# A gated recurrence on one Trainium2 core: level-0 fill ahead of the output step, output matrices in two buffers, output product in bank A

## What is computed

```python
def step(carry, inp):
    S, R = carry
    q_t, k_t, v_t, a_t, aR_t, b_t, g_t = inp
    kn = k_t / jnp.maximum(jnp.linalg.norm(k_t, axis=-1, keepdims=True), 1e-12)
    pred = jnp.einsum('bhji,bhj->bhi', S, kn)
    r = jnp.clip(v_t - pred, -CLIP, CLIP)
    S = a_t[..., None] * S
    kp = jnp.einsum('bhd,bhde->bhe', kn, S)
    S = S + b_t[..., None, None] * kn[..., None] * (v_t - kp)[..., None, :]
    o = jnp.einsum('bhji,bhj->bhi', S, q_t)
    R = aR_t[..., None] * R
    kpR = jnp.einsum('bhd,bhde->bhe', kn, R)
    R = R + g_t[..., None, None] * kn[..., None] * (r - kpR)[..., None, :]
    o = o + jnp.einsum('bhji,bhj->bhi', R, q_t)
    return ((S, R), o)
_, os = jax.lax.scan(step, (S0, S0), xs)
out = jnp.moveaxis(os, 0, 1).reshape(Bs, Ts, DI) @ Wo.T
return out + residual
```

## Time and profile before

| | |
|---|---|
| three executions | 2985.55 us median (2983.88 to 2993.01) |
| profiled execution | 2989.19 us, span of the core 2987.4 us |
| PE busy | 2398.5 us (80%), 49947 instructions |
| DVE busy | 1954.5 us (65%), 4625 |
| ACT busy | 1363.1 us (46%), 3250 |
| POOL busy | 1002.2 us (34%), 1250 |
| granted PE clock, mean over the span | 0.896 of full |
| gated recurrence | about 917 to 1980 us from the span's start |
| 12 runs of its loop | 1096.51 to 1820.20 us |

### The profile page before, as it was taken

One profiled execution on the slowest core, in us unless ns is written; L12 is line 12 of the kernel. 1 busy time (PEld: TensorE's weight loads), 2 busy tenths in 40 slices (PEclk: granted clock), 3 DMA queues, 4 the chain that ended last, 5 costly groups with the idle time before them and its releaser, 6 DMA issues. The chain is left out here.

```text
span 2987.4 us, 115613 instructions
## 1 busy us (share of the span) xinstructions
PE 2398.5 (80%) x49947; PEld 1861.7 (62%) x49947; DVE 1954.5 (65%) x4625; ACT 1363.1 (46%) x3250; POOL 1002.2 (34%) x1250
## 2 busy tenths in 40 slices
PE   8987478999976578888778887669998997797754
PEld 6754465555555577777777776548776654575633
DVE  3448335777756787888777888157777666564752
ACT  5443133444443344454444542447776553563420
POOL 0000324556650345434543355311111440360004
PEclk9979677999997799999999999969999998897876
DMA  3200331111110000000000000012221003242014
GB/s 99 66 1 29 114 116 53 47 47 46 47 58 3 3 4 4 4 4 4 4 4 4 4 4 4 3 27 61 63 62 58 4 3 108 64 110 66 5 43 122
DMA packets 80270, 117.47 MB, mean 39 GB/s; under 512 B 11490, under 2 KB 66034, under 8 KB 79234
## 3 DMA queue, kind: packets, MB, share of 16 engines
q1 hardware_dynamic: 71250, 100.31, 10.9%
q0 software_dynamic: 8576, 10.53, 1.7%
HBM read 98.16 MB, written 16.51 MB: 38 GB/s over the span
## 5 line engine op out<-in xcount | busy, mean ns | idle before, releaser
L2469 POOL TENSOR_SCALAR l1xs_p<-l1xs_p,l1xs_col 128x257 f32<-128x257 f32 x256 | 234.3, 936 | 204.4 <-DVE l1xs_col L2425 204.4
L3173 PE MATMUL psum<-l1d_rw,l1d_cols 64*32 64x48 f32 x16384 | 188.1, 211 | 106.1 <-issue 76.1
L3173 PEld LDWEIGHTS psum<-l1d_rw,l1d_cols 64*32 64x32 f32 x16384 | 164.4, 108 | 128.5 <-issue 118.1
L2390 ACT ACTIVATE l1xs_p<-psum,l1xs_col 128x257 f32<-128x257 f32 x256 | 119.7, 473 | 209.6 <-DVE l1xs_col L2420 203.5
L3429 DVE TENSOR_TENSOR l1d_rw<-l1d_rw,l1d_tots 128x1536 f32<-128x1536 f32 (+1 forms) x96 | 141.4, 1473 | 64.9 <-PE psum L3173 64.3
L2945 POOL TENSOR_TENSOR l1d_kc<-l1d_ms,l1d_beta 128x512 f32<-128x512 f32 x16 | 17.5, 1093 | 494.9 <-DVE l1d_ms L3484 477.9
L2432 DVE STREAM_TRANSPOSE l1xs_pt<-l1xs_p 128x288 f32<-128x288 f32 x256 | 122.4, 478 | 79.1 <-POOL l1xs_p L2469 79.0
L3112 PE MATMUL psum<-XN,l1d_wp 128*128 128x128 f32 x1024 | 142.6, 296 | 7.6 <-issue 6.7
L3112 PEld LDWEIGHTS psum<-XN,l1d_wp 128*128 128x128 f32 x1024 | 130.6, 206 | 21.0 <-issue 17.8
L2354 PE MATMUL psum<-l1xs_pt,l1xs_vals 32*128 32x512 f32 x1152 | 136.6, 604 | 0.0
L2342 PE MATMUL psum<-l1xs_keys,l1xs_qx 128*32 128x257 f32 x2048 | 132.7, 392 | 3.7 <-DVE l1xs_qx L2414 1.9
(11 more groups left out here) (563 smaller groups left out, 6852.7 us busy)
## 6 DMA issues: line engine op xcount, KB each, us to landing
l2f_w<-in_l2f_w SPq DMA_DIRECT2D x16, 768.0 KB
l1xs_vals<-in_ctx_strips SPq DMA_DIRECT2D x16, 576.0 KB
l0f_w<-in_l0f_w SPq DMA_DIRECT2D x15, 579.0 KB
l0x_ctxT<-in_ctxT SPq DMA_DIRECT2D x16, 516.0 KB, 3.7
l1xs_keys<-in_ctxT SPq DMA_DIRECT2D x16, 516.0 KB
l2x_ctxK<-in_ctxT SPq DMA_DIRECT2D x64, 129.0 KB, 2.1
l2x_ctxV<-in_ctxT SPq DMA_DIRECT2D x64, 129.0 KB, 2.1
l3f_w<-in_l3f_w SPq DMA_DIRECT2D x15, 193.5 KB
```

The costliest lines, as they stand in the source:

```text
L2390: nc.scalar.activation(p[:, t % 4, :S2], score_ps(t)[:, :S2], ACT.Exp, bias=col[:, 0, t % 4:t % 4 + 1], accum_out=col[:, 1, t % 4:t % 4 + ...
L2469: nc.gpsimd.tensor_scalar(p[:, t % 4, :S2], p[:, t % 4, :S2], col[:, 2, t % 4:t % 4 + 1], None, ALU.mult).then_inc(s["norm"], 1)
L3173: mm = nc.tensor.matmul(k.ps[bank0 + pr + e // per * 2][b * T:b * T + T, e % per * w:(e % per + 1) * w], columns[rr, at:at + T], moving[rr ...
```

## The change

Six edits, all in the gated recurrence:

1. On PE the level-0 fill of the next tile stands ahead of the output step.
2. ACT writes the two matrices of the output step for odd tiles into a second buffer, `wideN`, which lies in a buffer of the layer norm that is done by then; POOL clears it once. ACT's wait for the output product is then one tile later, both widenings move up, and the copy of the output step (rd) comes after the columns and the inverse.
3. The output projection of tile i-3 stands behind z, in pair A instead of B, and the last two tiles' stay at the end in bank 0.
4. DVE adds its result behind the first corner, no longer between the two level-0 keeps.
5. The key projection moves back behind the second S merge step, the aR gate behind the second R merge step; ACT takes u ahead of the keys.
6. Waits follow: u waits for the result addition instead of the keys, q for the copies of the output step, k for u.

```diff
--- before.py
+++ after.py
@@ -2840,6 +2840,8 @@
         ll = sb("ll", [128, 2, 2, H, T // 2])
         wideM, wideX = sb("wideM", [128, 5, H, 64]), sb("wideX", [128, 2 * H, 64])
         v, u, rd, ya = (sb(n, [128, 1024]) for n in ("v", "u", "rd", "ya"))
+        wideN = norm.bufs[5][:].rearrange("p c j d -> p (c j d)").rearrange("p (n h t) -> p n h t", n=2, h=H)
+        output = lambda i, j: wideM[:, j] if i % 2 == 0 else wideN[:, j - 1]
         kc, lt, xi = sb("kc", [128, T * T]), sb("lt", [128, T * (T + 1)]), sb("xi", [128, T * (T + 1)])
         tmp, wmat = sb("tmp", [128, 1024]), sb("wmat", [128, 128])
         block = ph.enter_context(nc.Block())
@@ -2853,7 +2855,7 @@
         bank_q = lambda i: 0 if i == 0 else bank("B")
         bank_gate = lambda i, n: (0, 2)[n] if i == 0 else bank("BA"[n])
         tokens = lambda i: k.XN[:, i * 128:(i + 1) * 128]
-        out_ps = lambda i: k.ps[bank("B") if i < NT - 2 else 0]
+        out_ps = lambda i: k.ps[bank("A") if i < NT - 2 else 0]
 
         @block.sync
         def _(sp):
@@ -2873,6 +2875,8 @@
             nc.gpsimd.memset(wideM[:], 0.0).then_inc(s["zero"], 1)
             pool.wait_ge(s["zero"], 2)
             nc.gpsimd.memset(xi[:, 0:T * T:T + 1], 1.0).then_inc(s["zero"], 1)
+            pool.wait_ge(norm.s["cols"], NCH)
+            nc.gpsimd.memset(wideN, 0.0).then_inc(s["zero"], 1)
             tt = nc.gpsimd.tensor_tensor
 
             def blocks(x, m):
@@ -3026,11 +3030,13 @@
                 x, f = ((ms, 1), (ms, 2), (mr, 0), (ll, 0), (ll, 1))[j]
                 needs = ("p_mm", "o_mm", "o_mm", "z_mm", "z2_mm")[j]
                 act.wait_ge(s["scaled"], i + 1)
-                if i > 0:
-                    act.wait_ge(s[needs], i * 2)
+                ahead = 1 if j in (1, 2) else 0
+                if i > ahead:
+                    act.wait_ge(s[needs], (i - ahead) * 2)
+                to = output(i, j) if ahead else wideM[:, j]
                 x = x[:, i % 2, f] if j >= 3 else x[:, i % 2, :, f, :]
                 for h in range(2):
-                    y = wideM[:, j, :, 32 * h + (16 if j >= 3 else 0):32 * h + 32]
+                    y = to[:, :, 32 * h + (16 if j >= 3 else 0):32 * h + 32]
                     sign = 2 if j in (0, 3, 4) else 0
                     ins = activation(y, x, ACT.Identity, scale=part[:, sign + h:sign + h + 1])
                 ins.then_inc(s["wideM"], 1)
@@ -3060,7 +3066,7 @@
             take_gate(0, 1)
             take_gate(0, 0)
             columns(0)
-            act.wait_ge(s["zero"], 3)
+            act.wait_ge(s["zero"], 4)
             for i in range(NT + 2):
                 old, mid, new = 0 <= i - 2 < NT, 0 <= i - 1 < NT, i + 1 < NT
                 if old and i <= NT:
@@ -3071,11 +3077,9 @@
                     take(i - 2, "y_mm", ya, "A", "y")
                     widen_x(i - 2, 1)
                     widen(i - 2, 4)
+                    take(i - 2, "u_mm", u, "A", "u")
                 if new:
                     take_k(i + 1)
-                if old:
-                    take(i - 2, "u_mm", u, "A", "u")
-                if new:
                     take_gate(i + 1, 1)
                 if old:
                     take(i - 2, "y2_mm", ya, "A", "y2")
@@ -3087,15 +3091,14 @@
                 if mid:
                     widen(i - 1, 3)
                     widen(i - 1, 0)
-                if old:
-                    take(i - 2, "o_mm", rd, "B", "o")
-                if mid:
                     widen(i - 1, 1)
                     widen(i - 1, 2)
                 if new:
                     columns(i + 1)
                 if mid:
                     widen_x(i - 1, 0)
+                if old:
+                    take(i - 2, "o_mm", rd, "B", "o")
                 if i == NT:
                     take(i - 1, "v_mm", v, "A", "v")
 
@@ -3117,14 +3120,14 @@
                 if i > 0:
                     pe.wait_ge(s["kn"], i * 2)
                 if i >= 3:
-                    pe.wait_ge(s["y"], i * 2 - 4)
+                    pe.wait_ge(s["u"], i * 2 - 4)
                 projected(i, 1, bank("A"), "k_mm")
 
             def project_q(i):
                 if i > 0:
                     pe.wait_ge(s["kn"], i * 2)
                 if i >= 4:
-                    pe.wait_ge(s["x"], i - 3)
+                    pe.wait_ge(s["o"], i * 2 - 6)
                 projected(i, 0, bank_q(i), "q_mm")
 
             def project_ar(i):
@@ -3234,13 +3237,13 @@
                 if i + 3 < NT:
                     pe.wait_ge(s["q"], i * 2 + 8)
                 elif i < NT - 1:
-                    pe.wait_ge(s["x"], i)
+                    pe.wait_ge(s["o"], i * 2)
                 apply(i, "B", wide(3), ya, "z_mm")
 
             def step_u(i):
                 pe.wait_ge(s["t"], i * 2 + 2)
-                if i + 3 < NT:
-                    pe.wait_ge(s["k"], i * 2 + 8)
+                if 0 < i < NT - 1:
+                    pe.wait_ge(s["x"], i)
                 apply(i, "A", inv(0), ya, "u_mm")
 
             def step_p(i):
@@ -3275,15 +3278,17 @@
                     for r in range(2):
                         rr = slice(64 * r, 64 * r + 64)
                         out = k.ps[bank("B") + r][64 * (h % 2):64 * (h % 2) + 64, h // 2 * 64:h // 2 * 64 + 64]
-                        nc.tensor.matmul(out, u[rr, h * 64:(h + 1) * 64], wideM[rr, 1, slot(h), :], start=True, stop=False)
-                        mm = nc.tensor.matmul(out, ya[rr, h * 64:(h + 1) * 64], wideM[rr, 2, slot(h), :], start=False,
+                        nc.tensor.matmul(out, u[rr, h * 64:(h + 1) * 64], output(i, 1)[rr, slot(h), :], start=True, stop=False)
+                        mm = nc.tensor.matmul(out, ya[rr, h * 64:(h + 1) * 64], output(i, 2)[rr, slot(h), :], start=False,
                                               stop=True)
                         if h == H - 1:
                             mm.then_inc(s["o_mm"], 1)
 
             def step_out(i):
                 pe.wait_ge(s["o"], i * 2 + 2)
-                if i >= NT - 2:
+                if i < NT - 2:
+                    pe.wait_ge(s["y"], i * 2 + 4)
+                else:
                     pe.wait_ge(s["mS"], NT * LEVELS)
                     pe.wait_ge(s["mR"], NT * LEVELS)
                 if i == NT - 1:
@@ -3312,10 +3317,10 @@
                     step_y(i - 2)
                 if now:
                     fill_s(i, 1)
-                if new:
-                    project_k(i + 1)
                 if old:
                     step_z(i - 2)
+                if 3 <= i <= NT:
+                    step_out(i - 3)
                 if now:
                     fill_r(i, 1)
                 if old:
@@ -3323,11 +3328,13 @@
                 if now:
                     fill_s(i, 2)
                 if new:
-                    project_ar(i + 1)
+                    project_k(i + 1)
                 if old:
                     step_p(i - 2)
                 if now:
                     fill_r(i, 2)
+                if new:
+                    project_ar(i + 1)
                 if old:
                     step_y2(i - 2)
                 if new:
@@ -3348,12 +3355,12 @@
                     broadcast(i + 1)
                 if now:
                     fill_r(i, 4)
-                if old:
-                    step_o(i - 2)
                 if new:
                     fill_0(i + 1, 0)
                     fill_0(i + 1, 1)
                 if old:
+                    step_o(i - 2)
+                if i >= NT:
                     step_out(i - 2)
                 if i == NT:
                     values(NT - 1)
@@ -3558,16 +3565,17 @@
                     turn(i - 1)
                 if now:
                     keep_s(i, 0)
-                if i >= 3:
-                    result(i - 3)
                 if now:
                     keep_r(i, 0)
                     advance_s(i, 0)
+                if now:
                     advance_r(i, 0)
                     advance_s(i, 1)
                     keep_s(i, 1)
                 if old:
                     corner(i - 2, "z_mm", v, "t")
+                if i >= 3:
+                    result(i - 3)
                 if now:
                     advance_r(i, 1)
                     keep_r(i, 1)
```

## The result

| | before | after |
|---|---|---|
| executions on the same chip | 2984.72 us median (2983.42 to 2993.01, 4 executions) | 3046.69 us median (3041.7 to 3055.43, 4 executions) |
| profiled execution | 2989.19 us, span 2987.4 | 3051.27 us, span 3049.3 |
| granted PE clock, mean over the span | 0.896 | 0.877 |

The ratio is 1.0224, with a 95% interval of 1.0201 to 1.0246 (that of the two medians alone, 1.0208, lies in it): the change makes the kernel slower, as forecast, but by 62 us by the medians and not by 33. The new median lies 0.7 us above the range. (Where the title says "output product in bank A", it is the output projection that moved to pair A.)

The account below looks back on a forecast made before the run. PE, going through its list in order, loses time between pieces as code arrives in blocks of 128 matmuls. Terms of -1.4 + 4.6 - 0.8 give +2.4 us per run, 31 in 13 runs, plus 2: 3018 us, range 2968 to 3046.

Parts of the forecast that it names:

- E to T, minus 1.4 us: Norm broadcast's end to next first S merge step: level-0 fill ahead of output step shortens it to 17.2 us.
- the clock behind the two new waits: PE at half clock after idling: 0.5 us counted for y2; output step 2.6 us at full clock or 3.6 at half.
- T to Y, plus 4.6: First S merge step to y2's start: projection 2.05, gate wait 2.7, result wait 0.3, less 0.5 us code time.
- The Trainium skill's drain: ACT's table switch ahead of y2: by the skill page a drain of about 1380 ns; not included in the sum.
- Y to E, minus 0.8: y2's start to norm broadcast's end: one stall back -1.0, half clock +0.5, shorter waits -0.3 us per run.
- The wait for the totals gone: At the first S merge step: PE's 1.2 us wait for DVE's totals disappears.
- Rest at nothing: Second output matrices, POOL memset and moved ACT copies cost nothing; last output projection after the loop adds 2 us.
- The sum per run: Whole loop run of the gated recurrence: -1.4 + 4.6 - 0.8 = +2.4 us.
- Rival (c): Idle stretches ahead of the fill and y2 bring half clock, with no run spared: 3042 us, chance 0.14.
- Rival (a): New PE idle time between first S merge step and y2 replaces issue stalls, making it faster: 2969 us, chance 0.22.
- What would show it: Profile signs: y2 and fill idle times, values to values 62 to 63 us, issue 5 or 6, loop clock below 0.95.

Follow-up runs that it names:

- run B: Not a separate kernel: one loop run in the changed kernel's profile, picked to show the two new PE waits; y2 starts after 2.80 us of idle PE.
- Experiment 10: Two variants of the kernel before: level-1 R merge step issued twice, 3041.9 us (1.0199); that step cut to its last head pair, 2969.77 us (0.994).
- experiment 7: Changed kernel with unread filler matmuls in one PE wait: only ahead of the level-0 fill, 3043.43 us (1.019); only ahead of y2, 3031.65 us (1.017).
- Experiment 5: Changed kernel with keys, aR gate and output step back in old places, output projection between y and first S merge step, result added earlier: 2979.55 us (1.0015).
- experiment 2: Changed kernel with only the first edit undone, the output step again ahead of the level-0 fill on PE: 3043.93 us (1.0208).

## Why the prediction was off

The direction and the case were right: slower, by a wait for ACT at y2 that nothing covers, and one more piece from T to Y. The size was 62 us where it said 33. Two terms failed: the gain that the swap was to give from E to T, minus 1.4 us per run, which came as plus 0.75; and the clock behind the two new waits, counted at 0.5 us per run (and a part of the output step's 1.0), which measured 2.3. By its own steps:

- **E to T, minus 1.4 us: wrong, and the main error.** The twelve runs show +0.75. The forecast had 17.2; it is 19.09. (Its 18.6 for the kernel before came from two runs, one of them with the stall below; all twelve give 18.34, so that 0.3 of the minus 1.4 was never there.) Its pieces: the fill starts 5.64 us after E on average, not 4.7; it takes 4.28 from its start to its end, not the 3.7 from 4.7 to 8.4 (7.3 + 1.1); and from its end to T 9.16, not 8.8. The first is mostly a stall in the code ahead of it, which the sum took away (it counted 7.3 without the wait of 1.34) although nothing in the change removes it: seven of the twelve fills start 4.9 to 5.2 us after E, five start 6.3 to 6.8. The second and third are the half clock: each half of the fill 1.75, and PE's path, not DVE's, ends the stretch. Against the kernel before, the swap had nothing to bring forward: the fill's second half starts 8.08 us after E in both kernels, for before it came only 0.3 us behind DVE's row 0, and now row 0 itself ends 0.25 later. From there on it is the clock: the second half takes 1.84 us for 1.39, and the path from its end to T 9.16 for 8.87, together the 0.75. The prediction had "the output step, 2.6 at full clock or 3.6 at half", and its 17.2 was near the lower end of the 16.9 to 17.9 that this gave. Rows of after, of one run with the stall:

```profile
1338.82 1.16 PE L3164 MATMUL psum<-l1d_small,l1d_hsel 32*128 32x128 f32 x16
1339.91 1.24 PE L3176 MATMUL psum<-l1d_rw,l1d_cols 64*32 64x32 f32 x123
1343.00 0.26 PE L3176 MATMUL psum<-l1d_rw,l1d_cols 64*32 64x32 f32 x5 [1.86 <-issue]
1346.82 1.75 PE L3176 MATMUL psum<-l1d_rw 64*32 64x112 f32 x64 [3.56 <-DVE l1d_rw L3404]
```

  Five matmuls of the level-4 step come 1.86 us late, DVE's keep waits for them, row 0 behind it, and the fill starts 6.84 us after E (run B: 5.02). The same stall was in the earlier trace rows, in one of the two runs that were read; in the kernel before it is in three runs of twelve. Experiment 10 shows the pace at which code arrives; why it strikes here in five runs of twelve was not measured.
- **T to Y, plus 4.6: right.** 4.3 measured: 1.9 more busy time for the projection's 2.05, and issue 0.3 less where 0.5 was counted. The wait for the gate is 2.6 us on average and 2.80 in run B, forecast 2.7. The upper bound (2.66 + 1.0) was not reached, since ACT again started at the half. The result's wait is 4.4 us in 5 times.
- **The Trainium skill's drain: not here.** The wait would have been an estimated 4.1 us by "ScalarE: Activation LUTs", section "What ACT_TABLE_LOAD costs". The load took 1.28 us, the first sigmoid began 0.01 us behind it, and the wait was 2.80: the trace disagrees with the 1380 ns of drain. It does so too for each run's other load, which starts 0.02 us behind ACT's instruction before it and has its first sigmoid 0.01 us behind as well.
- **Y to E, minus 0.8: wrong.** It is 0.0. The half clock behind y2's wait costs 1.0 us on average over the twelve runs (1.54 in run B), not 0.5. And the stall that was to come back here, 1.0, came back elsewhere: issue fell by 0.4 from Y to E, 0.3 from T to Y, and 1.2 from E to T, where the forecast had none, 2.0 in all for 1.5. PE's waits for DVE shrank by 0.7 for 0.3. The filler of experiment 7 at y2, which adds work and takes none away, shortened this stretch by 1.8.
- **The wait for the totals gone: right**, 12.1 to 0.2 us. That it gains nothing was the miss: it had marked DVE as the last to arrive at T, and now PE is.
- **Rest at nothing: nearly right.** Experiment 5's ratio of 1.0015 holds the second matrix buffer, the moved widenings and the late result, all of them within what can't be told from no change. The tail, +2 us, is not there: the twelve runs end 63.1 us late (1883.28 against 1820.20), the profiled executions 62.1.
- **The sum per run.** +2.4 forecast, +5.2 measured. Between the marks it is 2.65 more than forecast: 2.15 from E to T, 0.8 from Y to E, and 0.3 the other way from T to Y. By cause, 2.3 us per run of the measured 5.2 are the clock (PE's busy time), for which the forecast had counted 0.5 openly and a part of the output step's 1.0.
- **Rival (c), the clock, 3042 us, chance 0.14:** its mechanism is what happened, and its chance was too small. It priced the half clock at 1.7 to 1.9 us per run more than the forecast's 0.5, and 2.3 in all were measured. That its time comes within 5 us is partly luck: it kept the swap's gain, so it has some 4.2 us per run for the 5.2 measured, and counted 13 full runs and 2 us of tail where the twelve runs hold the whole difference. Its condition was that no run is spared any more, and hardly one is: y2 takes 2.81 us or more of PE's time in 11 of 12 runs (2 of 12 before), the first half of the fill 1.75 in 10 of 12. The same wait doesn't always bring the clock down: with it, y2 took 2.08 us in one run of the kernel after and in four of experiment 2. A wait that is there in every run still needs a chance of its own of bringing the clock down in nearly every run.
- **Rival (a), the fetch absorbs it, chance 0.22: wrong.** Relief was 2.0 us of issue per run, 0.5 more than the 1.5 forecast and short of the further 2.4 from which this rival decides. The mechanism exists (experiment 10), but the two new waits of a run together bought back some half of one block's time.
- **What would show it:** y2's idle time 2 to 3 us, ended by ACT's ar: right, 12 times in the twelve runs (10 of them in that span). Idle ahead of both halves of the fill, 3.4 and about 1.4: 3.55 and 0.71 in run B, the second shorter since the fill's first half ran at half clock. Values to values 62 to 63: missed, 65.5. Issue 5 to 6: 6.0. Clock below 0.95: 0.88.

## What to carry to other kernels

A wait that is short on paper cost twice here: once as idle time on TensorE, and again in the work behind it, which ran near 1.2 GHz. Put a price on the second from the same profile (PE's busy time over the same instructions, before and after), and give it to every wait that a change puts into every iteration. A step that another engine must drain before its bank is written again should have at least one piece of the other bank pair behind it: that alone was 36 us here, the clock's part included.

Read a stretch in as many repetitions as the trace has, not two. The stall that delays the fill is in five runs of twelve (three before), and the forecast had taken it off as if the change did that. And before work is moved forward to where an engine is idle, look at what the work behind it waits for: the fill's second half starts 8.08 us after E with the output step ahead of the fill and behind it, since DVE's row 0, for which it waits, came no sooner.

## What the hardware showed

- In run B 2.80 us of idle ahead of y2 were followed by a granted clock of 0.59, and 3.55 us ahead of the fill by 0.50 for 8.4 us. In the twelve runs the same matmuls kept PE busy for 27.4 us more. With the waits filled the ratio was 1.0113 for 1.0224, 33 us by the medians. The Trainium skill, "TensorE: Matmul & The Clock Gate", Part 1, puts the penalty of the ramp at a kernel's start at less than 1% of a typical kernel's span; here the clock falls again in nearly every iteration, and the ratios show 1.1 points.
- Five matmuls that nobody reads, added per run, made the kernel faster: 1.0224 to 1.0113. They were worth it only where PE was the last to arrive (at y2: 16 us; at the fill, where DVE's totals come next: 10 us, not clear of nothing).
- An added 1.3 us of matmuls cost 3.6 us. It fits a reading in which 128 recorded matmuls are a block of code that arrives as one packet of the instruction queue, once in 3.8 us between two restarts, 4.1 on average: 12 more such steps brought 12 more packets. Idle time elsewhere bought it back only in part in the changed kernel: PE's waits for DVE and ACT grew by 4.9 us per run, and issue fell by 2.0.
- Taking nearly the same out gained a third of that, with PE and DVE each idle for a fifth of the stretch: the busy shares alone did not show how little was to be had.

Not tried: the stall in the level-4 step by itself (a kernel with fewer matmuls between the broadcast and the fill), and the gate's spacing together with the filler at the fill. No version with the full result beats the kernel before; the nearest, experiment 5, can't be told from it.
